# Three transposing transfers per chunk, gate r's pair products in the order P7, P1, P5, P6, and a finer start

## What is computed

```python
Af, AfT = A.astype(f32), A.T
state = x
for _ in range(5):
    s_in, s_out = state @ in_W.T + in_b, state @ out_W.T + out_b
    a_in, a_out = Af @ s_in, AfT @ s_out
    a = concatenate([a_in, a_out, state], axis=-1)
    r = sigmoid(a @ r_W.T + r_b)
    z = sigmoid(a @ z_W.T + z_b)
    joined = concatenate([a_in, a_out, r * state], axis=-1)
    h_hat = tanh(joined @ h_W.T + h_b)
    state = (1.0 - z) * state + z * h_hat
out = tanh(state @ o1_W.T + o1_b) @ o2_W.T + o2_b
x = layernorm(x + out)
```

## Time and profile before

| | |
|---|---|
| median of three executions | 993.23 us |
| the profiled execution | 991.49 us |
| its span (first to last instruction) | 989.7 us |
| TensorE busy | 966.8 us (98%) |
| VectorE busy | 736.6 us (74%) |
| ScalarE busy | 456.1 us (46%) |
| chain that ended last: share on TensorE | 90% |
| mean granted TensorE clock | 0.995 |

### The profile page before, as it was taken

One profiled execution on the slowest core, in us unless ns is written; L12 is line 12 of the kernel. 1 busy time (PEld: TensorE's weight loads), 2 busy tenths in 40 slices (PEclk: granted clock), 3 DMA queues, 4 the chain that ended last, 5 costly groups with the idle time before them and its releaser, 6 DMA issues.

```text
span 989.7 us, 11827 instructions
## 1 busy us (share of the span) xinstructions
PE 966.8 (98%) x4480; PEld 441.1 (45%) x4480; DVE 736.6 (74%) x1154; ACT 456.1 (46%) x640; POOL 36.3 (4%) x43
## 2 busy tenths in 40 slices
PE   6999999999999999999999999999999999999995
PEld 3444444444444444444444444444444444454443
DVE  4999979888886587756757776776676686645756
ACT  3757665553354346423634553363345335421443
POOL 0310100000000000000000000000000020001100
PEclk9999999999999999999999999999999999999998
DMA  9998995234720454284025607601570582032101
GB/s 332 393 412 346 395 330 129 60 80 106 213 64 1 128 149 97 32 214 128 1 80 154 139 12 176 167 19 40 152 166 15 132 226 62 1 108 84 44 1 43
DMA packets 199112, 134.34 MB, mean 136 GB/s; under 512 B 61712, under 2 KB 191376, under 8 KB 194960
## 3 DMA queue, kind: packets, MB, share of 16 engines
q1 hardware_dynamic: 196752, 125.20, 43.8%
q0 software_dynamic: 2304, 8.39, 2.2%
HBM read 102.11 MB, written 16.78 MB: 120 GB/s over the span
## 4 chain that ended last, share of the span: by engine, by line
PE 90%; DVE 4%; ACT 2%; issue 1%; DMA 1%; SPq 1%; ACTq 0%; DVEq 0%
PE bank L1746 36%; PE bank L1875 19%; PE bank L1854 12%; PE bank L1676 11%; PE bank L1867 6%; PE bank L1886 4%; PE bank L1967 1%; DMA tmp<-in_adj 1%; PE bank L1946 1%; ACT areg L708 1%; SPq L378 0%; DVE pq_words L1073 0%; DVE tmp L968 0%; ACT sop_words L571 0%; ACT pq_words L607 0%
## 5 line engine op out<-in xcount | busy, mean ns | idle before, releaser
L1746 PE MATMUL bank<-areg,xop_words 128*128 128x512 fp8e4 x1792 | 389.4, 379 | 2.0 <-issue 1.8
L1746 PEld LDWEIGHTS bank<-areg,xop_words 128*128 128x128 f16 x1792 | 174.7, 98 | 214.3 <-issue 3.2
L708 ACT ACTIVATE areg<-pq_words 128x512 f16<-128x512 f32 x90 | 56.3, 629 | 174.8 <-DVE pq_words L1317 72.0
L1875 PE MATMUL bank<-areg,pq_words 128*128 128x512 f16 x504 | 119.2, 379 | 0.7 <-DVE areg L1353 0.7
L1676 PE MATMUL bank<-areg,xop_words 128*128 128x512 fp8e4 x512 | 113.2, 382 | 3.2 <-ACT areg L542 3.2
L1875 PE MATMUL bank<-areg,w 128*128 128x512 f16 x378 | 90.9, 379 | 1.4 <-DVE areg L1353 1.4
L1353 DVE SCALAR_TENSOR_TENSOR areg<-pq_words,areg 128x512 f16<-128x512 f32 x90 | 62.7, 697 | 32.4 <-ACT areg L708 30.6
L1676 PEld LDWEIGHTS bank<-areg,xop_words 128*128 128x128 f16 x512 | 50.1, 98 | 65.4 <-issue 7.0
L542 ACT ACTIVATE areg<-tmp 128x2048 fp8e4<-128x2048 int32 x32 | 61.1, 1911 | 34.2 <-DMA tmp<-in_adj 17.5
L1875 PEld LDWEIGHTS bank<-areg,pq_words 128*128 128x128 f16 x504 | 49.2, 98 | 60.4 <-DVE areg L1353 1.2
L1854 PE MATMUL bank<-pq_words,w 128*128 128x512 f16 x288 | 65.4, 379 | 0.0
(11 more groups left out here) (209 smaller groups left out, 1205.7 us busy)
## 6 DMA issues: line engine op xcount, KB each, us to landing
areg<-kept_operands SPq DMA_DIRECT2D x112, 512.0 KB, 4.3
tmp<-in_adj SPq DMA_DIRECT2D x16, 1024.0 KB, 7.0
tmp<-in_adj_t SPq DMA_DIRECT2D x16, 1024.0 KB, 8.4
kept_operands<-xop_words POOLq DMA_DIRECT2D x11, 512.0 KB, 8.0
areg<-in_x SPq DMA_DIRECT2D x8, 512.0 KB, 6.6
kept_operands<-areg SPq DMA_DIRECT2D x4, 1024.0 KB, 9.8
kept_operands<-tmp POOLq DMA_DIRECT2D x5, 512.0 KB, 3.2
pq_words<-in_gate_w SPq DMA_DIRECT2D x6, 384.0 KB, 6.1
```

Of the source, the lines that this page charges most:

```text
L708: nc.scalar.activation(y_dst(t, g, name)[:, 0, :], src, ACT.Copy, scale=PSC).then_inc(s_yh, 1)
L1746: last = nc.tensor.matmul(dst[:, :], xop[:, m // 2, operand_block(xo, part, m % 2), :], place8[:, mo, m, :], start=first and m == pairs[0] ...
L1875: last = nc.tensor.matmul(dst[:, :], weights(d, wp), yop[:, d, Y_PLACE[name], xp, :], start=False, stop=final and d == 1 and (wp, xp) == P ...
```

## The change

1. **Gate r opens in another order** (`pair_gate` on TensorE): P7, P1, P5, P6, all behind one wait for the four bias terms. Gates z and h keep P1, P6, P5, P7. VectorE's and ScalarE's programs of a pair unit, `pair_gates` in front, are the same but for two moved calls at the end of a p = 1 unit (3).
2. **Three transposing transfers per chunk**: part f = 1 is laid out as ten hi blocks and ten lo blocks, each turned by a transfer of its own; the hi blocks are sent when ScalarE has written them. `rows_hi` of f = 1 is split into block 22 and the sums.
3. **Order around a new step**: the transfers go chunk by chunk; the third chunk's sums are written before the pair unit's last activations and updates, and `first_group` has 16 more matmuls to do ahead of its last wait.
4. **Start**: x comes in five parts, the first adj row in two halves with a cast and a semaphore each, weights' evictions are both ahead of the first cast, and x is split in parts of 1, 3, 4, 4, 4 tiles. The first pass takes banks in numerical order. `matrix_sums(3)` moves behind `make_diag(0)`, and most of `degree_differences` from step 1's start to chunk 1 of step 0.

```diff
@@ pair_gate, TensorE
-                pe.wait_ge(s_c1, seeds + 1)
-                pair_product(t, p, gate, slots[0], "y11", block(0, 0)).then_inc(s_gp1, 1)
-                pe.wait_ge(s_c1, seeds + 2)
-                pair_product(t, p, gate, slots[1], "t2", block_sum(2)).then_inc(s_gp6, 1)
-                pe.wait_ge(s_c1, seeds + 3)
-                pair_product(t, p, gate, slots[2], "t1", block_sum(1)).then_inc(s_gp5, 1)
-                pe.wait_ge(s_c1, seeds + 4)
-                pair_product(t, p, gate, slots[3], "t3", block_sum(3)).then_inc(s_gp7, 1)
+                if gate == 0:
+                    pe.wait_ge(s_c1, seeds + 4)
+                    pair_product(t, p, gate, slots[3], "t3", block_sum(3)).then_inc(s_gp7, 1)
+                    pair_product(t, p, gate, slots[0], "y11", block(0, 0)).then_inc(s_gp1, 1)
+                    pair_product(t, p, gate, slots[2], "t1", block_sum(1)).then_inc(s_gp5, 1)
+                    pair_product(t, p, gate, slots[1], "t2", block_sum(2)).then_inc(s_gp6, 1)
+                else:
...
@@ turn_rows, SP
+                for n in range(CH * t, CH * (t + 1)):
+                    sp.wait_ge(s_xl, part_done(n, 0))
+                    need(sp, s_p4, 4 * t)
...
+                    turn(n, 0)
+                    sp.wait_ge(s_xh, part_done(n, 1))
+                    turn(n, 1)
+                    sp.wait_ge(s_xl, part_done(n, 1))
+                    turn(n, 2)
@@ first_group, TensorE
-                early, late = (range(6), (6, 7)) if t == 1 else (range(4), (6, 7, 4, 5))
-                wait_turned(pe, 0, n - len(late) // 2)
+                early, next_rows, late = (range(6), (), (6, 7)) if t == 1 else (range(4), (6, 7), (4, 5))
+                before = n - len(next_rows + late) // 2
+                wait_turned(pe, 0, before)
...
                 product(bank_f, at, XS3, MT3, early[:-2], final=False)
+                if t > 1:
+                    wait_turned(pe, 0, n - 1)
+                    product(bank_a, at, X11, M11, next_rows, first=False, final=False)
+                    wait_turned(pe, 1, n - 1)
+                    product(bank_b, at, XS2, MT2, next_rows, first=False, final=False)
+                    product(bank_e, at, XS1, MT1, next_rows, first=False, final=False)
                 wait_turned(pe, 0, n)
                 product(bank_a, at, X11, M11, late, first=False).then_inc(s_p1, 1)
                 product(bank_f, at, XS3, MT3, early[-2:], first=False, final=False)
+                if t > 1:
+                    product(bank_f, at, XS3, MT3, next_rows, first=False, final=False)
+                    product(bank_c, at, XS4, M22, next_rows, first=False, final=False)
@@ pair_gates of p = 1, ScalarE, then VectorE
                     rows_hi(CH * t + 2, 0)
+                    rows_hi_x22(CH * t + 2)
                 pair_act(t, p, 2, 2)
+                if p == 1:
+                    rows_hi_sums(CH * t + 2)
                 pair_act(t, p, 2, 3)
                 if p == 1:
                     rows_hi(CH * t + 3, 0)
-                    rows_hi(CH * t + 2, 1)
                     rows_hi(CH * t + 3, 1)
...
                 pair_update(t, p, 2)
+                if p == 1:
+                    rows_lo(CH * t + 2, 1)
                 pair_update(t, p, 3)
                 if p == 1:
                     rows_lo(CH * t + 3, 0)
                     row_sums(CH * t + 3)
-                    rows_lo(CH * t + 2, 1)
                     rows_lo(CH * t + 3, 1)
@@ start
+X_PARTS = ((0, 4), (4, 8), (8, 12), (12, 14), (14, 16))
+HI_PARTS = ((0, 1), (1, 4), (4, 8), (8, 12), (12, 16))
...
+            def cast_first_row():
+                half_n = N // 2
+                act.wait_ge(s_row0, 16)
+                nc.scalar.activation(a8[:, 0, 0:half_n], stage[:, 0, 0:half_n], ACT.Copy,
+                                     accum_out=mx[:, 5:6], saturate=False).then_inc(s_cast0, 1)
+                act.wait_ge(s_adj[0], 16)
+                nc.scalar.activation(a8[:, 0, half_n:], stage[:, 0, half_n:], ACT.Copy,
+                                     accum_out=mx[:, 6:7], saturate=False).then_inc(s_cast, 1)
...
             fold_out(0)
-            cast_rows(0)
             fold_out(1)
+            cast_first_row()
```

More of the change, by code:

```diff
@@ L186, in gnn_program @@
         s_xt = [sem("s_xt0"), sem("s_xt1")]
-        s_x = [sem(f"s_x{c}") for c in range(CH)]
+        s_x = [sem(f"s_x{i}") for i in range(len(X_PARTS))]
+        s_row0, s_cast0 = sem("s_row0"), sem("s_cast0")
         s_adj = [sem(f"s_adj{i}") for i in range(STG)]
@@ L318, in wait_turned @@
         def wait_turned(eng, f, n):
-            for b in range(2):
-                need(eng, s_turn[f][b], 16 * turns(n, b))
+            for part in ((1, 2) if f else (0,)):
+                for b in range(2):
+                    need(eng, s_turn[part][b], 16 * turns(n, b))
         def p0_bank(c, f):
@@ L347, in turn_parts @@
             ns = range(CH * t, CH * (t + 1))
-            if t == 0:
-                return [(n, f) for n in ns for f in range(FT)]
-            return [(ns[0], 0), (ns[0], 1), (ns[1], 0), (ns[1], 1), (ns[2], 0), (ns[3], 0), (ns[2], 1), (ns[3], 1)]
+            return [(n, f) for n in ns for f in range(FT)]
         def part_done(n, f):
@@ L594, in rows_hi @@
                     act.wait_ge(s_new, state_done(at, 0))
-                    for part in range(2):
+                    for part in range(3):
                         need(act, s_turn[part][turn_slot(n)], 16 * turns(n - 1, turn_slot(n)))
@@ L899, in link @@
                 dve.wait_ge(s_sc, chain[0])
-            for c in range(CH):
-                dve.wait_ge(s_x[c], 16)
-                last = nc.vector.tensor_reduce(mx[:, 8 + c:9 + c], x_nat[:, c * JC:(c + 1) * JC, :],
+            for i, (lo, hi) in enumerate(X_PARTS):
+                dve.wait_ge(s_x[i], 16)
+                last = nc.vector.tensor_reduce(mx[:, 7 + i:8 + i], x_nat[:, lo:hi, :],
                                                mybir.AxisListType.XY, ALU.max, apply_absolute_value=True)
             link(last)
-            nc.vector.tensor_reduce(mx[:, 0:1], mx[:, 8:12], AX, ALU.max).then_inc(s_mx, 1)
+            nc.vector.tensor_reduce(mx[:, 0:1], mx[:, 7:12], AX, ALU.max).then_inc(s_mx, 1)
             dve.wait_ge(s_mall, 1)
@@ L911, in _ @@
             link(nc.vector.tensor_scalar(SIG, T1, TOP, None, ALU.mult))
[L912 to L916, removed]
+            for i, (lo, hi) in enumerate(HI_PARTS):
+                nc.vector.tensor_scalar(state_n[:, lo:hi, 0, :], x_nat[:, lo:hi, :], SIG, None, ALU.mult) \
+                    .then_inc(s_snh, 1)
+                dve.wait_ge(s_snh, i + 1)
+                for j in range(lo, hi):
                     nc.vector.scalar_tensor_tensor(state_n[:, j, 1, :], x_nat[:, j, :], SIG, state_n[:, j, 0, :],
@@ L994, in make_diag @@
                 dve.wait_ge(s_cast, JT if d == 0 else 2 * JT)
+                if d == 0:
+                    link(nc.vector.tensor_tensor(degc[:, 0, 0:1], mx[:, 5:6], mx[:, 6:7], ALU.add))
                 for j in range(JT):
@@ L997, in make_diag @@
                 last.then_inc(s_diag, 1)
-            for i in range(4):
+            for i in range(3):
                 matrix_sums(i)
@@ L1016, in _ @@
             make_diag(0)
-            for i in range(4, PAIRS):
+            for i in range(3, PAIRS):
                 matrix_sums(i)
@@ L1672, in _ @@
                                             start=ct == 0, stop=ct == FT - 1)
-                last.then_inc(s_fold, 1)
+                    if ct == FT - 1 and (lo == 0 or k == FT - 1):
+                        last.then_inc(s_fold, 1)
             def adj_mm(dst, adj8, j, part, f, c):
@@ L1681, in _ @@
                 pe.wait_ge(s_snl, j + 1)
-                pe.wait_ge(s_cast, j + 1)
-                for b in (0, 1, 4, 6, 7, 2, 3, 5):
+                if j == 0:
+                    pe.wait_ge(s_cast0, 1)
+                else:
+                    pe.wait_ge(s_cast, j + 1)
+                for b in (0, 1, 2, 3, 4, 5, 6, 7):
                     if j == 0 and b == 2:
                         pe.wait_ge(s_fev, 2)
+                    if j == 0 and b == 4:
+                        pe.wait_ge(s_cast, 1)
                     for part in range(2):
@@ L1797, in first_group @@
                 product(bank_a, at, X11, M11, early, final=False)
-                wait_turned(pe, 1, n - len(late) // 2)
+                wait_turned(pe, 1, before)
                 if t > 1:
```

87 lines of the change are left out of this document (53 added, 34 removed).

## The result

The changed kernel takes 998.0 us (median of 4 runs, 997.1 to 999.7) against 992.5 for the kernel before (4 runs): ratio 1.0067, 95% interval 1.0055 to 1.008. It is slower by 6.6 us, with 5.5 to 7.9 as the interval; 999.6 had been predicted, with a range of 993 to 1004.5.

What follows compares the result with a forecast made beforehand. TensorE bounds the kernel, busy 966.8 of 989.7 us. Order +10.4, first unit -0.2, first groups -1.8 and start -2.0 give +6.4: 993.23 becomes 999.6 us; range 993 to 1004.5.

Steps and rivals of the forecast that it cites:

- The order, six units: Gate r's new opener order makes VectorE's chain 1.85 us late; gate z pays 1.74 us in six units, +10.4 us.
- the first unit: Step 1, p = 0: openers end some 1.9 us sooner, chain relatively 1.85 later; -0.2 us, between -0.4 and +0.4.
- (a): Gate r: pair_sum_12 ends after y22's product wants it, a stall of 0.2 to 0.3 us.
- (b): Everything behind pair_sum_22 is 1.85 us late, through ScalarE's L764 and the ping-pong up to gate z.
- 13 or 14 entries: Sign: TensorE's waits get a row for L1520 with this many, some 10 us in total, longest near 1.5.
- The start: First adj matmul 1.2 us sooner, plus half of 1.5 us from the clock: -2.0 us, from 0 to -2.7.
- later adj rows don't come sooner: Bound on the start's gain: if this holds, the gain is 0 instead of -2.0 us.
- First groups: Steps 2 to 4: all three waits for transposing transfers go, -1.8 us; at worst 0, +1 if an added wait binds.
- The edits at nothing: Moved degree differences (0.75 us at most without cover), moved matrix_sums(3) and step 1's first group: no effect.
- A: Rival: the chain into gate z has slack absorbing the 1.85 us; only gains of -4.0 remain, 989.2 us; chance 0.09.
- B: Rival: only half the units pay, p = 0 units unchanged; +1.2 us, 994.4 us; chance 0.08.
- C: Rival: TensorE's clock falls in gate z's new waits of 1.5 us; +9 us, 1008.6 us; chance 0.06.

Runs made afterwards that it cites:

- e7: Kernel before with only the three transposing transfers per chunk and the new first-group order of steps 2 to 4: 991.1 us against 991.2, ratio 0.9997.
- e6: Kernel before with only the start's edits (smaller first loads, halved first cast, new fold evictions, adj columns in order): 989.8 us against 991.2, ratio 0.9983.
- e1: Changed kernel with gate r's openers back in the order P1, P6, P5, P7: 988.5 us against 991.6 for the kernel before, ratio 0.9967.
- e3: Changed kernel with t4's low half put ahead of U on VectorE: 996.3 us against 991.6 for the kernel before, ratio 1.0051.
- e4: Changed kernel with gate r's openers as P7, P1, P6, P5: 990.3 us against 991.6 for the kernel before, ratio 0.9994.
- e8: Changed kernel with P7, P1, P6, P5 only in step 1, p = 0, and P1, P6, P5, P7 in the other six units: 987.0 us against 991.2, ratio 0.9957.

## Why the prediction was right

**The order, six units.** Predicted 1.74 each and 10.4 together. The trace has 1.69 to 1.70 and 10.2; taken out, it is 9.9, done alone 10.8 (both with the first unit, predicted -0.2, measured -0.3). Its steps held: U starts 0.20 behind the fourth opener, the shift is 1.81 where 1.85 was taken, and gate z gets all of it but 0.12. The 0.04 are a misread row: in the earlier trace rows L1520 starts 0.70 behind L1353 only because it waits for P5, whose successor starts at 375.91, 0.20 before it; VectorE's own pace is 0.60. (a) and (b) don't add, as said: (a) is 0.22 of the 1.69. One sign came out otherwise: 13 or 14 entries were expected in TensorE's own row, and there are seven, since gate r's 0.22 hardly exceed the 0.16 that such a row hides; the fourteen are in the weight loads' row. This term alone carries the verdict, and the earlier trace rows with the earlier trace rows were enough to find it.

**The start.** Predicted -2.0: 1.2 from the cast and half of the clock's 1.5. Alone it was -1.7 (-3.4 to 0), within the bounds. In the profiled pair the lead is 21.04 - 19.59 = 1.45 us at the first matmul; the clock came back wholly, so that it grows to 23.90 - 21.09 = 2.81 at the eighth. But it is 84.08 - 82.26 = 1.82 at the first diagonal block, 135.12 - 134.15 = 0.97 at step 0's gates, and 0.56 at step 1, of which the last 0.4 are the degree terms of e7. The prediction named a bound for this (later adj rows don't come sooner) and gave it no weight. e6 still has 2.16 at step 1, so the loss isn't fixed. In e1, which kept 0.46, it is seen that late rows take the lead: the cast waits for a row, and TensorE for the cast.

```profile
124.30 1.91 ACT L565 ACTIVATE areg<-tmp 128x2048 fp8e4<-128x2048 int32 x1 [1.96 <-DMA tmp<-in_adj_t]
...
126.36 1.90 PE L1717 MATMUL bank<-areg,xop_words 128*128 128x512 fp8e4 x8 [0.94 <-ACT areg L565]
```

**First groups.** Predicted -1.8, and this is the term that was mis-sized: -0.8 by the rows of e7, -0.3 (-1.2 to +0.6) by its time. The waits for transfers went as worked out. Two things were missed. Four of the sixteen matmuls put ahead of the wait had covered VectorE's sum of y22, which now costs 0.2 us in each of three steps; step 1 of the kernel before had that wait. And ScalarE's split `rows_hi`, with its new semaphore wait, makes step 0's degree terms 0.2 late twice; e6, without that split, waits for them as before (0.4 against 0.5 us). "At worst 0" did hold.

**The edits at nothing.** The moved degree differences weren't run alone. e1 has all parts but the order and is 3.3 us faster than before; e6 and e7 add up to 2.0, with intervals of 1.7 and 0.9 us, so the 1.3 left may be chance. The traces leave the moved differences nothing: from the first gates of step 0 to step 1 the lead of e1 falls from 0.87 to 0.46, and e7 loses the same 0.4 without them; from there to gate z's slot 1 product of step 1, p = 0 e1 takes 301.20 - 228.69 = 72.51 us, against 301.67 - 229.15 = 72.52.

**The rivals.** A, slack in the chain: refuted by the seven waits of 1.3, and by e3 and e4, where the length of the unit follows the shift to 0.1 us. B, half the units: the p = 0 units of steps 2 to 4 wait just as long. C, the clock: it stays at 1.00 through every wait on L1559, and the span's mean is 0.998. The Trainium skill, "TensorE: Matmul & The Clock Gate", section "A second HAM failure mode: psum-queue depth-cycling", had made C the likely case: it tells of idles between groups of matmuls that are frequent enough to make the clock swing. Here seven waits of up to 1.3 us in 998 us left the granted clock at 1.00; so few of them are hardly the frequent ones it speaks of.

**The sum.** Predicted +6.4, measured +6.6 by the ratio. This match is in part luck. The measured terms give 10.1 - 0.3 - 0.8 for order, unit and first groups, and 1.7 (time) to 2.16 (trace) for the start of e6: +6.8 to +7.3, inside the interval of 5.5 to 7.9, which hides that the first groups were 1 us too good. Within the start two errors offset: clock and first matmul brought 2.8 and not 2.0, and late rows took 0.7 of it back in e6. Also, the prediction's own range of +5 to +10.5 isn't what its bounds add up to: with 10.7, +0.4 and +1 the upper end is above +12.

## What to carry to other kernels

When products are reordered on one engine, list what the next engine still has to do when the last of them is through, and how long that is; here it went from one operation to four and cost 1.7 us a unit. Here a wait of 0.2 us repeated in every unit, and the links before it alternated between two engines; that chain had 0.12 us of slack, and any further delay was paid in full. When matmuls are moved ahead of one wait, look at what they covered where they stood; an order that suits one late unit belongs in that unit alone (e8).

## What the runs showed of the hardware

Two 128x512 f32 additions of VectorE start 0.60 us apart when the second doesn't read the first's output (L1559 and L1564 in the changed kernel), though each lasts about 0.69. Where it does read it and waits for its semaphore, they start 0.80 apart (U and L1559 in e3) or 0.72 (L1525 at 378.06 and L1527 at 378.78 in the kernel before); why these two differ is not shown. On ScalarE such a wait between two operations moved the second from 0.40 to 0.58 us behind the first (e7).

TensorE's granted clock kept its upper level of 2.4 GHz through idles of 1.3 and 1.8 us with work on both sides, and was at the lower of 1.2 after one of 3.18. The length of the last idle alone doesn't decide it: at the start of e7 one of 2.56 us was followed by a granted clock of 0.50, and at the start of e3 one of 2.74 by 1.00.
